# x1's batches two groups sooner, and gamma and the last addition on GpSimd, in a two-layer graph network

## The reference

```python
h = relu(layernorm(x))
m = relu(concat([h[src], edge_attr]) @ W_msg.T + b_msg)
m = relu(m @ W_msg2.T + b_msg2)
h_neigh = segment_sum(m, dst) / max(count, 1)
x = x + concat([h, h_neigh]) @ W_apply.T + b_apply          # this is x1

h = relu(layernorm(x))
alpha = segment_softmax(edge_weight, dst)
agg = normalize(segment_sum(alpha * h[src], dst))
comb = normalize(0.5 * (h @ W_self + b_self + agg @ W_nb + b_nb))
x = x + layernorm(comb) * gamma + beta
```

## Time and profile before

| | us |
|---|---|
| median of three runs | 9611.87 |
| profiled execution | 9613.47 |
| its span, first to last instruction | 9611.7 |
| busy: TensorE, VectorE, ScalarE, GpSimd | 6155.9, 3553.0, 1122.0, 6169.5 |
| GpSimd's gathers of layer 0 | first at 92.7, last at 4907.8 |
| GpSimd's gathers of layer 1 | first at 4967.7, last at 9546.6 |

### The profile page before, as it was taken

One profiled execution on the slowest core, in us unless ns is written; L12 is line 12 of the kernel. 1 busy time (PEld: TensorE's weight loads), 2 busy tenths in 40 slices (PEclk: granted clock), 3 DMA queues, 4 the chain that ended last, 5 costly groups with the idle time before them and its releaser, 6 DMA issues.

```text
span 9611.7 us, 88594 instructions
## 1 busy us (share of the span) xinstructions
PE 6155.9 (64%) x26549; PEld 4562.7 (47%) x26549; DVE 3553.0 (37%) x12551; ACT 1122.0 (12%) x2108; POOL 6169.5 (64%) x6486
## 2 busy tenths in 40 slices
PE   5777877788888888888864444445444544544545
PEld 4555555555555555555553333333333333333335
DVE  5334333333333333333353333333333333333336
ACT  3111211111111111111130000000000000000002
POOL 4666666666666666666656666666666666666664
PEclk8878887888888888878876666665656565556566
DMA  5222222222333333222222222211111111111112
GB/s 168 68 62 64 68 66 64 69 68 75 79 81 79 80 79 74 68 70 68 68 75 59 59 57 59 54 47 47 47 47 47 47 47 47 47 47 47 47 47 83
DMA packets 353136, 618.73 MB, mean 64 GB/s; under 512 B 125106, under 2 KB 227550, under 8 KB 338846
## 3 DMA queue, kind: packets, MB, share of 16 engines
q0 software_dynamic: 206336, 422.99, 17.3%
q1 hardware_dynamic: 133134, 183.58, 7.6%
q10 hardware_dynamic: 13200, 6.56, 0.2%
HBM read 576.76 MB, written 35.92 MB: 64 GB/s over the span
## 4 chain that ended last, share of the span: by engine, by line
POOL 44%; PE 20%; issue 18%; another core or an unknown queue 10%; DMA 4%; DVE 3%; ACT 1%; SPq 0%; DVEq 0%; ACTq 0%; POOLq 0%
POOL rows_ring L493 44%; PE bank L1065 9%; PE bank L1127 6%; PE bank L1124 3%; DMA rows_ring<-p_table,idx 2%; PE bank L1062 1%; PE bank L1180 1%; DMA rows_ring<-h_table,idx 1%; DVE acc L886 1%; DVE xq L711 0%; DVE acc L711 0%; ACT work L581 0%; DVE acc L999 0%; ACT work L587 0%
## 5 line engine op out<-in xcount | busy, mean ns | idle before, releaser
L493 POOL DMA_INDIRECT rows_ring<-p_table,idx x3224 | 3091.1, 959 | 1815.4 <-issue 861.0
L493 POOL DMA_INDIRECT rows_ring<-h_table,idx x3224 | 3062.3, 950 | 1535.4 <-issue 933.1
L886 DVE TENSOR_TENSOR acc<-acc,bank 128x128 f32 (+1 forms) x4836 | 1578.0, 326 | 5913.5 <-remote 3402.1
L1180 PE MATMUL bank<-work,rows_ring 128*128 128x256 f32 x4832 | 1618.5, 509 | 1811.2 <-DMA rows_ring<-h_table,idx 1679.6
L1180 PEld LDWEIGHTS bank<-work,rows_ring 128*128 128x128 f32 x4832 | 1261.9, 303 | 2164.1 <-DMA rows_ring<-h_table,idx 1824.7
L889 DVE TENSOR_SCALAR onehot<-iota,dloc,coef 128x128 f32<-128x128 f32 x4032 | 1413.3, 363 | 11.5 <-ACT coef L558 9.4
L1065 PE MATMUL bank<-wmat,work 128*128 128x128 f32 x6848 | 1195.4, 316 | 281.6 <-issue 277.8
L1065 PEld LDWEIGHTS bank<-wmat,work 128*128 128x128 f32 x6848 | 1139.3, 228 | 343.1 <-issue 302.8
L1065 PE MATMUL bank<-onehot,work 128*128 128x128 f32 x6448 | 1080.9, 315 | 155.5 <-issue 134.8
L1065 PEld LDWEIGHTS bank<-onehot,work 128*128 128x128 f32 x6448 | 984.6, 229 | 209.9 <-issue 208.5
L1127 PE MATMUL bank<-work,we_sb 64*128 64x512 f32 x1612 | 1067.5, 745 | 19.6 <-issue 19.0
(11 more groups left out here) (123 smaller groups left out, 1068.7 us busy)
## 6 DMA issues: line engine op xcount, KB each, us to landing
work<-in_edge_t SPq DMA_DIRECT2D x202, 512.0 KB
rows_ring<-p_table,idx POOLq DMA_INDIRECT x3224
rows_ring<-h_table,idx POOLq DMA_INDIRECT x3224
ht_rows<-rows_ring SPq DMA_DIRECT2D x25, 256.0 KB, 2.3
p_table<-rows_ring SPq DMA_DIRECT2D x25, 256.0 KB, 2.5
work<-ht_rows SPq DMA_DIRECT2D x25, 256.0 KB
h_table<-work ACTq DMA_DIRECT2D x25, 256.0 KB
work<-h_table SPq DMA_DIRECT2D x25, 256.0 KB
```

Of the source, the lines that this page charges most:

```text
L493: pool.indirect_dma_start(out=rows_ring[:, 16 * h + G * k + j, :], out_offset=None, in_=table[:, :], in_offset=bass.IndirectOffsetOnAxis(a ...
L886: dve.tensor_tensor(win, win, ps_sum[layer][k % slots][:, j * P:(j + span) * P], ALU.add).then_inc(added, 1)
L1180: ins = pe.matmul(ps_sum[1][slot][:, first:first + P * (1 + j % 2)], rows_ring[:, G * k + j, :], hot, start=j % 2 == 1, stop=j % 2 == 0)
```

## The change

Four edits:
- `X0_AT` becomes 786, so all x1 steps of layer 0 stand two slots sooner in the programs of TensorE, VectorE and ScalarE.
- In ScalarE's `x1_step` the batches from 20 on come five steps behind and no longer six.
- From batch 8 on (`POOL_AT`), gamma and the sum with x1 are done by GpSimd, two `tensor_tensor` of 128x512 behind its last gathers, each batch with a wait for ScalarE's and VectorE's rows, for its own multiply and for the free output buffer. VectorE leaves both out there, and SyncE's stores wait for GpSimd.
- For the same batches ScalarE scales and shifts three tiles and VectorE the fourth, at step s for batch s - 9, as one `tensor_scalar`.

The diff, without the line that names the three new semaphores (`fourth2_ready`, `late_scaled`, `late_fin_ready`):

```diff
@@ -46,7 +46,8 @@
 PARTS = 8
 FINAL = [min(T, (E - N + (c + 1) * G * P - 1) // P + 1) for c in range(NBATCH)]
 X1_AT = -(-FINAL[0] // G) + 3
-X0_AT = X1_AT + 2
+X0_AT = X1_AT
+POOL_AT = 8
 LAST_BODIES = X1_AT // 8
 BIG = 3.4028234e38
 LN_EPS = 1e-5
@@ -437,7 +438,10 @@
                 sp.dma_start(four(self_in[c % 4]), table_rows(self_rows, c)).then_inc(S2["self_loaded"][c % 4], 16)
 
             def store_out(c):
-                sp.wait_ge(S["fin_ready"], c + 1)
+                if c < POOL_AT:
+                    sp.wait_ge(S["fin_ready"], c + 1)
+                else:
+                    sp.wait_ge(S["late_fin_ready"], c - POOL_AT + 1)
                 done = S2["out_stored"][c % 4]
                 if (c + 1) * G > NTF:
                     for t in range(c * G, NTF):
@@ -510,6 +514,15 @@
                 pool.wait_ge(S2["h2_stored"][h], 16 * used(2, h))
             for i in range(NBODY + 1):
                 gather(1, h_table, i)
+
+            for c in range(POOL_AT, NBATCH):
+                rows4 = four(acc[:, c * G * P:(c + 1) * G * P])
+                pool.wait_ge(S["rows2_ready"], c + 1)
+                pool.wait_ge(S["fourth2_ready"], c - POOL_AT + 1)
+                pool.tensor_tensor(rows4, rows4, over4("gamma"), ALU.mult).then_inc(S["late_scaled"], 1)
+                pool.wait_ge(S["late_scaled"], c - POOL_AT + 1)
+                pool.wait_ge(S2["out_stored"][c % 4], 16 * (c // 4))
+                pool.tensor_tensor(four(fin[c % 4]), rows4, xq[:, c * G:(c + 1) * G, :], ALU.add).then_inc(S["late_fin_ready"], 1)
 
 
         @block.scalar
@@ -593,8 +606,7 @@
                     if chunk[-1] == s - 3:
                         act.wait_ge(S["var1_ready"], n + 1)
                         act.activation(columns(sc_a, chunk), columns(var, chunk), ACT.Sqrt, bias=eps[:, :], scale=1.0 / P).then_inc(S["root1_ready"], 1)
-                c = s - 6
-                if 0 <= c < NBATCH:
+                for c in [c for c in range(NBATCH) if c == s - (6 if c < 20 else 5)]:
                     h, n = c % 2, [c in chunk for chunk in CHUNKS1].index(True)
                     act.wait_ge(S["scale1_ready"], n + 1)
                     if c >= 2:
@@ -612,7 +624,7 @@
 
             bodies(act, layer0, {at_step[4]: exponentials})
 
-            for s in range(8 * (NPOOL + 1) - X0_AT, NBATCH + 6):
+            for s in range(8 * (NPOOL + 1) - X0_AT, NBATCH + 5):
                 x1_step(s)
             fill(1)
 
@@ -658,7 +670,7 @@
                 c = s - 9
                 if 0 <= c < NBATCH:
                     act.wait_ge(S["scale2_ready"], c + 1)
-                    for at in range(c * G, c * G + G):
+                    for at in range(c * G, c * G + (G if c < POOL_AT else G - 1)):
                         tile = acc[:, at * P:(at + 1) * P]
                         ins = act.activation(tile, tile, ACT.Identity, bias=mean[:, at:at + 1], scale=sc_b[:, at:at + 1])
                     ins.then_inc(S["rows2_ready"], 1)
@@ -959,7 +971,13 @@
                 def batch_at(lag):
                     return s - lag if 0 <= s - lag < NBATCH else None
 
-                inv, raw, arg, scl, gam, fin_c = (batch_at(lag) for lag in (2, 4, 6, 8, 10, 11))
+                inv, raw, arg, scl, one, gam, fin_c = (batch_at(lag) for lag in (2, 4, 6, 8, 9, 10, 11))
+                if one is not None and one < POOL_AT:
+                    one = None
+                if gam is not None and gam >= POOL_AT:
+                    gam = None
+                if fin_c is not None and fin_c >= POOL_AT:
+                    fin_c = None
                 parts_of = {c: [stat6[:, c * G:(c + 1) * G, j] for j in range(6)] for c in (raw, inv) if c is not None}
                 if inv is not None:
                     root = four_of(sc_a, inv)
@@ -981,6 +999,11 @@
                     marks["diff"] = order.mark(dve.tensor_tensor(diff, me, mo, ALU.subtract))
                     marks["parts"] = order.mark(dve.tensor_tensor(both_parts, se, so, ALU.add))
                     marks["mu"] = order.mark(dve.tensor_tensor(mu, me, mo, ALU.add))
+                if one is not None:
+                    dve.wait_ge(S["scale2_ready"], one + 1)
+                    at = one * G + G - 1
+                    tile = acc[:, at * P:(at + 1) * P]
+                    dve.tensor_scalar(tile, tile, sc_b[:, at:at + 1], mean[:, at:at + 1], ALU.mult, ALU.add).then_inc(S["fourth2_ready"], 1)
                 if gam is not None:
                     dve.wait_ge(S["rows2_ready"], gam + 1)
                     rows4 = four(acc[:, gam * G * P:(gam + 1) * G * P])
```

More of the change, by code:

```diff
@@ L184, in gnn @@
             squares_ready norms_in_psum norm_root_ready nb_in_psum u_ready
-            scalar_order unit_arg_ready unit_root_ready var2_ready root2_ready scale2_ready rows2_ready scaled_ready fin_ready""".split()
+            scalar_order unit_arg_ready unit_root_ready var2_ready root2_ready scale2_ready rows2_ready scaled_ready fin_ready fourth2_ready late_scaled late_fin_ready""".split()
         S = {n: sem(n) for n in names}
```

## The result

| | before | after |
|---|---|---|
| median, runs beside each other | 9615.81 (9609.63 to 9623.85, 6 runs) | 9656.35 (9636.09 to 9663.53, 6 runs) |
| profiled execution, its span | 9613.47, 9611.7 | 9654.49, 9652.7 |
| busy: TensorE, VectorE, ScalarE, GpSimd | 6155.9, 3553.0, 1122.0, 6169.5 | 6152.9, 3556.4, 1116.5, 6196.4 |

The change costs 40.5 us: ratio 1.0042, interval 1.0028 to 1.0053. The six runs of before include the three of the forecast. The forecast was 9625, its range ended at 9641. Busy times hardly move, but for GpSimd's new work; what grew is idle time.

The account below looks back on a forecast made before the run. Bounds taken: GpSimd's gathers and TensorE in turns at layer 0's end, then VectorE and ScalarE; VectorE in the tail. 2.6 + 0.9 + 4.4 + 5.3 = +13.2 us on 9611.9 gave 9625, range 9600 to 9641.

Parts of the forecast that it names:

- The slot of 5.20 us: End of layer 0: TensorE's product starts 0.71 us later, making a 4.49 us slot 5.20, 0.20 over the gathers.
- 20 slots at 0.20 and 4 at 0.98: End of layer 0: cost of TensorE waiting for VectorE's first addition of the same slot, 7.9 us over 24 slots.
- The gain of 5.3 in the drain: From layer 0's last sums to layer 1's first gather: 5.1 us from two x1 batches less, 0.2 from ScalarE.
- Part 2: Tail: GpSimd takes gamma and x1 from batch 8 on, VectorE the fourth tile; forecast +0.9, +4.4 and +5.3 us.
- T: Tail: length of one GpSimd tensor_tensor of 128x512, taken as 1.2 us, between 0.62 and 1.37.
- 0.9 + 4.4 = 5.3: Tail: steps 17 and 18 cost +0.9 us; steps 19 to 26, at 4.5 instead of 3.95, cost +4.4.
- The closing: Tail after step 26: GpSimd holds 7 more batches of 2.65 us, 20.5 us against 15.2, +5.3.
- SyncE's queue: Tail: stores from batch 8 on wait for GpSimd, with batch 24's self-row load behind store 9; costed at nothing.
- (c): Rival, end of layer 0: TensorE sets the pace and pays the whole wait, +18.2, with the tail +28.8: 9641; chance 0.22.
- part 1: End of layer 0: x1 two slots sooner, 7.9 cost less 5.3 gain, +2.6 us, between -5.3 and +18.2.
- (b): Rival, both places: GpSimd's instruction is near the copy's length and TensorE's wait is covered, -12 us: 9600; chance 0.17.
- (d): Rival, both places: no change, ScalarE eats the two slots, GpSimd's work falls into VectorE's gaps: 9612; chance 0.11.

Follow-up runs that it names:

- x0_alone_again: Only the x1 steps two slots sooner, against the kernel before, on chip 3: 8419.31 us in one run, beside 8402.33.
- before_again: The kernel before, unchanged, traced once more on chip 4, where it takes 8403.89 us.
- x0_alone: Only the x1 steps two slots sooner, against the kernel before, on chip 1: 9643.03 us beside 9619.19, ratio 1.0026.
- after_again: The whole change run again on chip 5, against the kernel before: 9758.13 us beside 9724.94, ratio 1.0033.
- act_alone: Only ScalarE's batches from 20 on one step sooner, against the kernel before: 9620.52 us beside 9619.19, ratio 0.9998.
- x0_one_slot: x1 steps one slot sooner instead of two, the rest as in the kernel before: 9615.33 us beside 9619.19, ratio 0.9997.
- x0_no_edges: x1 two slots sooner, edge loads from group 784 on and TensorE's waits for them left out, against the kernel before: 9734.68 us, one run.

## Why the prediction was wrong

- **The slot of 5.20 us was right** (5.23), and so was its reason.
- **What failed is the count "20 slots at 0.20 and 4 at 0.98", 7.9 us.** It took the gathers for the pace-maker in most slots, from the 0.51 us between 4.49 and 5.0. The measured cost is 24.3 us in 16 slots. The slack was there but was already spent: on this kind of chip five late results of some 6 us fall into the stretch, and TensorE won part of them back with its short slots. With 5.23, over the gathers' 5.0, it can't, so the short slots pay the whole 0.74. The slot of the late result grows too, since TensorE no longer runs on there (10.3 to 11.0 instead of 8.0 to 9.6), and so does the one at the lower clock behind it (9.4, once 6.6, instead of 6.2 to 8.7). Three such runs of four slots take 29.4 us on the mean instead of 25.6, which is 15 of the 24.3 for sixteen slots; the rest lies in the first slots of the stretch and is not split up. The row that said so was there, GpSimd's "remote" 11.4 and the bank's 10.5 in the earlier trace rows: the gathers were not without gaps. Even the bound of 23.5 for all 24 slots was passed. On the chips where the gathers do set the pace the price in these slots was zero (x0_alone_again and before_again, 80.1 both); in x0_alone_again TensorE's one long stand, 8.27 us, came behind them, in the drain.
- **The gain of 5.3 in the drain was too large.** With two slots it was 2.2 (after) and 3.4 (x0_alone), and not seen in after_again. Part of the reason is in the same wait: two slots just behind the first gather of group 805 take 5.2 and 6.9 us where they took 4.5 and 5.3. With one slot the drain gained 5.5. One trace each, and act_alone's drain is 5 us off without a known reason, so these differences are weak.
- **Part 2 by its steps.** T was 1.26 (1.2 taken). L967 to L999 took 0.90 with neither gamma nor sum; the forecast was 1.17 with the fourth tile at 0.26, which cost next to nothing, hidden among short ones. The step was 4.53 (4.5). From the last gather to the L1013 (L1036 in after) of the last full step it was +5.0, where 0.9 + 4.4 = 5.3 were forecast. The closing, from the start of that instruction to the end of the last addition, took 9647.8 - 9625.25 = 22.5 us against 9609.3 - 9594.0 = 15.3, +7.2 where +5.3 was forecast: the period of 2.56 us was right (2.65), but VectorE's small operations and its fourth tile stood up to 1.2 to 1.4 us beside GpSimd and left it gaps at the start. (The prediction calls 9593.96 the end of L1013; it is its start. And by its own 2.05 + 2T the step turns at T = 0.95, not 0.92. Neither moves the forecast.)
- **A term put at nothing: the program's end.** The prediction's closing ended with the last addition, as if the rest stayed the same. It grew from 2.4 to 4.9 us, by GpSimd's DRAIN: +2.5. These three, 5.0 + 7.2 + 2.5, are the tail's 14.7.
- **SyncE's queue** cost nothing that shows, as taken.
- **The rivals.** (c), chance 0.22, had the mechanism: TensorE pays the whole wait, +18.2 for part 1; measured +20.2 from group 782 to layer 1, and 23.8 alone. Its 9641 was short by the tail's 4.1 and by what differs ahead of group 782. (b) and (d) didn't happen. The chance of slower by over 0.2% should have been the largest.

The sum: 13.2 forecast, 40.5 measured. By the runs of each part alone 21 us are missing in part 1 (2.6 against 23.8) and 7 in part 2 (10.6 against 17.6), together 28, within the noise of the 27 that the whole change misses.

## What to carry to other kernels

Slack between two engines is free only if nobody draws on it: read not the median slot but the slow ones, and ask how their time is won back, for a wait that fits into every fast slot can still take away the recovery. Before moving a wait, list what is queued behind it; here moving the product behind the next slot's transposes removed the loss, and one slot instead of two never had it. Work given to an idle GpSimd beside a VectorE full of small two-input operations costs by where they meet, not by GpSimd's idle time: a tail step took 3.95 us with VectorE doing both operations, 4.53 with both on GpSimd, and 3.60 with one there, beside the statistics. And let another engine do the last work of a program: GpSimd's end cost 2.5 us more.

## What the runs showed of the hardware

- Chips differ by kind: 9616 to 9726 us and 8402 to 8404 for one kernel. On the first kind 604 results of TensorE came late by the trace (3402 us of VectorE's waits), on the second none; GpSimd's gathers take 0.95 to 0.96 us each on both. What causes them is open. Edge loads aren't it (four in x0_no_edges); the one case with a single one had TensorE's slots at 6.6 us.
- After standing 6.2 us TensorE was granted 0.52 of its clock on the mean, the lower level, for 9.4 us, and eight products took 2.08 us instead of 1.16; after 8.3 us in x0_alone_again they took 2.07.
- A program whose last work is GpSimd's ended 4.9 us behind it, with a DRAIN of 5.85 to 5.97 us (five traces); where it was VectorE's, 2.4 us behind it (fifteen).
- GpSimd's tensor_tensor of 128x512 takes 1.26 us, 2.0 times the copy of 0.62. The Trainium skill (GPSIMD Engine Reference, Elementwise — side-by-side cycle accounting) led to an estimate of 1.12; the measurement decides.
- A VectorE instruction can be kept out for a whole row of GpSimd's instructions: it stood 8.85, 8.43 and 8.23 us beside rows of 17 or 18 copies and 7.59 beside 17 writing ones. It need not be: in the other traces VectorE's operations got in between the copies (0.52 each in the earlier trace rows, 0.74 at most in x0_one_slot).
